# A four-layer graph network on one core: the tables that feed its list scheduler, and the order of its preparation, are replaced

## The reference

```python
deg_inv_sqrt = jnp.where(deg > 0, jax.lax.rsqrt(deg), 0.0)          # deg = adj.sum(axis=1)
x = _layernorm(x + norm_adj @ (x @ W0) + b0)                         # layer 0
o = softmax(mask(q @ k.T * scale)) @ v @ w_proj + b_proj             # layer 1: 8 heads, mask from adj
x = _layernorm(x + o + layernorm(o) * gamma + beta)
for _ in range(3):                                                   # layer 2: a gated unit, 3 steps
    z = sigmoid(av @ w3.T + h @ u3.T); r = sigmoid(av @ w4.T + h @ u3.T)   # av = [adj @ h, adj @ h]
    h = (1 - z) * h + z * tanh(av @ w5.T + (r * h) @ u5.T)
x = _layernorm(x + h)
x = _layernorm(x + softmax(q @ k.T / sqrt(32) + (1 - adj) * -1e9) @ v @ Wo + bo)   # layer 3
```

## Time and profile before

| what | value |
|---|---|
| median of 3 runs | 2582.63 us (2581.03 to 2584.98) |
| the profiled execution | 2584.22 us |
| its span in the trace | 2582.4 us, 1.8 us less than its own time |
| TensorE busy | 2531.3 us, 98% of the span |
| VectorE, ScalarE, GpSimd busy | 75%, 74%, 30% |
| mean granted TensorE clock | 0.997 |

### The profile page before, as it was taken

The page is one execution under the profiler, slowest core; times in us unless marked ns, Lnnn a source line. Parts: engine busy times, 40 slices in busy tenths (PEclk is TensorE's granted clock), DMA queues, the critical chain, the costliest instruction groups (busy, mean ns, idle before and its releaser), DMA issues.

```text
span 2582.4 us, 50299 instructions
## 1 busy us (share of the span) xinstructions
PE 2531.3 (98%) x17384; PEld 2052.0 (79%) x17384; DVE 1930.7 (75%) x5562; ACT 1913.1 (74%) x4322; POOL 775.7 (30%) x1086
## 2 busy tenths in 40 slices
PE   6999999999999999999999999999999999999997
PEld 5877787888878878788888888888788787787876
DVE  6867958769587785867868688695877858776776
ACT  3858848869597786968869597695977858684777
POOL 4323331323323222242323323233232322324221
PEclk9999999999999999999999999999999999999999
DMA  4212212122121222303122031221212223021122
GB/s 143 51 27 53 49 40 58 40 56 52 46 64 32 54 51 51 71 19 73 32 64 58 22 76 42 54 52 46 64 32 54 50 51 71 19 52 27 32 58 60
DMA packets 91083, 132.15 MB, mean 51 GB/s; under 512 B 15921, under 2 KB 40146, under 8 KB 90834
## 3 DMA queue, kind: packets, MB, share of 16 engines
q1 hardware_dynamic: 90834, 128.94, 21.0%
HBM read 19.83 MB, written 8.39 MB: 11 GB/s over the span
## 4 chain that ended last, share of the span: by engine, by line
PE 90%; DVE 5%; ACT 2%; issue 1%; POOL 1%; DMA 0%; SPq 0%; DVEq 0%; ACTq 0%; POOLq 0%
PE bank L1389 18%; PE bank L1390 17%; PE bank L1391 17%; PE bank L1446 16%; PE bank L1461 9%; PE bank L1438 8%; PE bank L1466 2%; PE bank L1499 1%; PE bank L1429 1%; ACT probs L940 1%; DVE probs L1179 1%; ACT res L977 1%; DVE PT L1190 0%; DVE vh L1245 0%; DVE gate L1156 0%
## 5 line engine op out<-in xcount | busy, mean ns | idle before, releaser
L940 ACT ACTIVATE probs<-probs,few 128x512 f32<-128x512 f32 x1024 | 731.4, 720 | 61.8 <-DVE few L1179 59.7
L1179 DVE CUSTOM_DVE_ANT_0 probs<-bank,mask 128x512 f32<-128x512 f32 x1024 | 668.5, 685 | 81.0 <-PE bank L1446 50.0
L1446 PE MATMUL bank<-ident,probs 128*128 128x128 f32 x4096 | 582.5, 273 | 7.4 <-ACT probs L940 5.3
L1446 PEld LDWEIGHTS bank<-ident,probs 128*128 128x128 f32 x4096 | 484.5, 141 | 84.1 <-issue 13.8
L1438 PE MATMUL bank<-stack 96*128 96x512 f32 x1024 | 419.8, 453 | 1.1 <-DMA stack<-qk 0.3
L949 ACT ACTIVATE PT<-bank 128x512 f32<-128x512 f32 x673 | 371.8, 596 | 37.1 <-PE bank L1446 31.6
L1190 DVE COPY PT<-bank 128x512 f32<-128x512 f32 x351 | 235.1, 682 | 49.4 <-PE bank L1466 30.5
L1389 PE MATMUL bank<-feat,W 128*128 128x512 f32 x640 | 259.1, 405 | 0.0
L846 POOL TENSOR_TENSOR feat<-o,feat 128x256 fp32r<-128x256 f32 x128 | 95.3, 744 | 527.6 <-ACT feat L962 526.3
L1390 PE MATMUL bank<-feat,W 128*128 128x512 f32 x640 | 253.3, 396 | 0.0
L1391 PE MATMUL bank<-feat,W 128*128 128x512 f32 x640 | 253.2, 396 | 0.0
(11 more groups left out here) (110 smaller groups left out, 5074.7 us busy)
## 6 DMA issues: line engine op xcount, KB each, us to landing
stack<-qk SPq DMA_DIRECT2D x768, 128.0 KB, 2.4
res<-in_x_dram SPq DMA_DIRECT2D x16, 512.0 KB, 3.8
out_dram<-res SPq DMA_DIRECT2D x16, 512.0 KB, 3.0
rows<-bo_sum SPq DMA_DIRECT2D x15, 128.0 KB, 2.9
rows<-in_L_gnn_bias_dram SPq DMA_DIRECT2D x14, 128.0 KB, 2.9
rows<-in_L_gnn_ln_beta_dram SPq DMA_DIRECT2D x14, 128.0 KB, 2.9
PT<-in_adj_dram SPq DMA_DIRECT2D x1, 1024.0 KB, 5.3
vh<-in_L_gnn_w_w_dram SPq DMA_DIRECT2D x2, 512.0 KB, 9.4
```

The lines of the kernel that those rows point to most:

```text
L940: k = act.activation(p, p, ACT.Exp, bias=least[:, t % P_RING:t % P_RING + 1], scale=-1.0, accum_out=sums[:, grp % 2, q * HG + h:q * HG + h ...
L1179: k = dve.tensor_tensor_reduce(out=probs[:, t % P_RING, :], in0=place("scores", t)[:, :], in1=mask[:, half * QT + q, :], scale=1.0, scalar ...
L1446: k = pe.transpose(place("transpose", t)[:, m * P:(m + 1) * P], probs[:, t % P_RING, m * P:(m + 1) * P], ident[:, :])
```

## The change

The numbers of the scheduler are replaced, and with them nearly every row of every engine's order moves. Beside that:

- `TO_PE`: TensorE sees what other engines produce 0.2 us later than others do, in the scheduler alone.
- `RANK` is another table, with kinds of its own for the first batches' pieces (`first ...`) and for each piece of preparation (`prep ...`).
- `mask3` is made on VectorE and the bias columns `cols` on GpSimd (each was on the other engine), and both masks come after batch 0 has been scaled.
- x of batch 2 is loaded with the first two. To free its place, the raw `u3` and `u5` lie in a part of `feat2` (`raw_us`); the first high half that overwrites it waits until they are turned.
- 17 transposes of the identity (`warm`), which no one reads, follow the row sums on TensorE.

```diff
+WARM = 17
-LATE = {"scores": 0.13, "stt": 0.11, "exp": 0.25, "transpose": 0.28, "pt": 0.25, "recip": 0.2, "rsum": 0.2, "values": 0.25,
+LATE = {"scores": 0.13, "stt": 0.11, "exp": 0.05, "transpose": 0.28, "pt": 0.13, "recip": 0.22, "rsum": 0.1, "values": 0.28,
+TO_PE = 0.2
-RAW_US = {"adj": (0.6, 4.6), "w0": (0.6, 2.5), "rows": (1.2, 2.0), "qkv1": (0.6, 3.5), "gru": (3.0, 5.0), "rest": (3.0, 5.0),
+RAW_US = {"adj": (0.6, 4.9), "w0": (0.6, 6.7), "rows": (1.2, 3.0), "qkv1": (0.6, 8.4), "gru": (4.0, 9.0), "rest": (4.0, 8.7),
...
-                ready = max([done[a] for a in piece.after], default=0.0)
+                late = TO_PE if piece.engines == ("PE",) else 0.0
+                ready = max([done[a] + (late if taken[a] != "PE" else 0.0) for a in piece.after], default=0.0)
                 if piece.opens:
-                    ready = max(ready, sorted(free)[len(piece.opens) - 1])
+                    ready = max(ready, sorted(free)[len(piece.opens) - 1] + late)
...
-    for name in ("adj", "x0", "w0", "x1", "qkv1", "rest", "gru", "small", "rows"):
+    for name in ("adj", "x0", "w0", "x1", "x2", "qkv1", "rest", "gru", "small", "rows"):
...
-    add("masks", "DVE", ("prep", "DVE", "mask1"), ("raw", "adj"))
-    add("masks_pool", "POOL", ("prep", "POOL", "mask3"), ("prep", "POOL", "pow"))
+    add("masks", "DVE", ("prep", "DVE", "mask1"), ("prep", "DVE", "dinv"), ("dve", "scale", 0, NT - 1))
+    add("masks", "DVE", ("prep", "DVE", "mask3"))
+
+    add("warm", "PE", ("prep", "PE", "warm"), ("prep", "DVE", "deg"), opens=[("warm", 0)], frees=[("warm", 0)])
...
-    add("biases", "DVE", ("prep", "DVE", "cols"), ("raw", "small"), ("raw", "rows"))
+    add("biases_pool", "POOL", ("prep", "POOL", "cols"), ("raw", "small"), ("raw", "rows"))
...
+                if name[:2] == ("ax", 2):
+
+                    wait_full(act, "turn", "u3")
+                    wait_full(act, "turn", "u5")
...
+                elif what == "warm":
+                    wait_free(pe, "warm", 0)
+                    pe.wait_ge(prep_pool.sem, prep_pool.at("ident"))
+                    pe.wait_ge(prep_dve.sem, prep_dve.at("some"))
+                    for i in range(WARM):
+                        k = pe.transpose(place("warm", 0)[:, 0:P], ident[:, :], ident[:, :])
+                    fill(k, "warm", 0)
```

More of the change, by code:

```diff
@@ new lines @@
+FIRST = ("scale", "ax", "w0", "n0", "rstd", "x1T", "q", "k", "v", "beta")
+def kind_of(key):
+    kind, what = key[:2]
+    if kind == "prep":
+        return f"prep {key[2]}"
+    if kind in ("pe", "act", "dve", "pool"):
+        b = key[2]
+        if what in FIRST and b < STREAMS and (what not in ("q", "k", "v") or key[3] == 1) and (
+                what != "rstd" or key[3] == "n0"):
+            return f"first {what} {b}" if what in ("scale", "ax", "w0") else f"first {what}"
+        return f"{kind} {what}"
+    if kind == "load" and what < STREAMS:
+        return "first load"
+    return f"values {key[2]}" if kind == "values" else kind
```

89 lines of the change are left out of this document (47 added, 42 removed), and 3 rows, old and new, of the table RANK.

## The result

The changed kernel takes 2589.73 us (median of 9 runs), the kernel before in the same comparison 2584.13 us (9 runs). The ratio is 1.0027, 95% interval 1.0018 to 1.0035: **slower by 0.27%**, where I had forecast 2575.5 us and given "slower" a chance of 0.11. The profiled execution has a span of 2587.9 us, 5.5 more than before. One of the nine runs took 3134 us at a mean granted clock of 0.751 and is left out of the ratio.

What follows compares the result with a forecast made beforehand. TensorE's order, idle time and half-clock work were taken to bound the kernel: 2582.4 - 8.3 + 3.3 - 0.5 - 1.5 = 2575.4 us of span, forecast as 2575.5 us. Range 2562 to 2585.

Steps and rivals of the forecast that it cites:

- slower: Rival, steady part: x3T waits as its chain gets 1.5 us longer, 12 batches lose 18: about 2593; chance 0.12.
- What bounds the kernel: Whole kernel: TensorE, busy 2531.3 of 2582.4 us; only its other 51 us and half-clock work can be won.
- that work was filler: Between batch 0's proj1 and x2T: TensorE work now done earlier had filled the norm chain; 6.0 us longer idle without it.
- a wait of over 5 us before batch 0's x2T: Sign expected in the profile after: TensorE waits that long ahead of these transposes.
- Start of ax: Opening: TensorE's first `ax` starts at 14.0 instead of 22.53, 8.5 us earlier.
- What is late next: Opening: weights wait for GpSimd's sums behind three scales from 23.2; w3 at 34.6, w5 at 39.2 us.
- Sum of the opening: Up to the first tile, at 65.0 with 12.1 us more work done: gain 8.3 us, bounds 11.2 or nothing.
- The middle of the opening: Batch 0's proj1 to x2T: 6.0 us more idle, 2.7 off for the norm; 3.3 us worse, bounds 0 and 6.
- Steady part: Repeating blocks: same TensorE work per batch, denser short blocks; 0.5 us better, bounds 6 either way.
- The end: Last block gets two more pieces of TensorE work, half of `proj3` moves later; 1.5 us better, bounds 0 and 3.
- It comes to nothing: Rival: scales cost near 6.22 us, or the chain to x2T is slow at half clock; say 2580; chance 0.26.
- two signs of being wrong: Bias row lands early in the opening, or a steady-part batch takes over 0.5 us longer.

Runs made afterwards that it cites:

- experiment 2: Kernel before with its own preparation, but the changed kernel's tables, ranks and later TensorE sight (`TO_PE`): 2593.0 us, ratio 1.0042.
- Experiment 1: Changed kernel plus one edge: q and k matmuls of layer 1 of batch 2 may not start before proj1 of batch 0: 2584.9 us, ratio 1.0009.
- Experiment 6: Changed kernel's preparation and opening ranks, with the kernel before's durations, delays and ranks for batch and tile work, `TO_PE` 0: 2581.9 us, ratio 0.9998.
- experiment 3: Changed kernel's preparation with the durations, delays and ranks of the kernel before: 2623.3 us, ratio 1.0161.
- experiment 7: Changed kernel with only TensorE's later sight (`TO_PE`) set from 0.2 to 0: 2639.0 us, ratio 1.0219.
- experiment 5: Kernel before plus one edge: proj1 of batch 0 waits for the last k matmul of layer 1 of batch 2: 2586.85 us, ratio 1.0016.

## Why the prediction was wrong

*What bounds the kernel* was right: TensorE's order and its idle time decide, and all differences lie there. The spent filler was named too, "that work was filler", and the sign to look for, "a wait of over 5 us before batch 0's x2T", is there with 5.42 us.

*Start of ax*: 14.0 forecast, 13.64 measured. *What is late next*: scales from 23.2 forecast, 23.6 measured; w3 at 34.6 against 32.94, w5 ready near 39.2 against sums that end by 36.7. I had added 2.9 us for shared time; the three scales took 7.95, 2.65 each instead of 2.40, so GpSimd lost 0.75 in all. VectorE lost more: its low halves of 0.67 took 2.40 and 2.27 beside the scales. The Trainium skill ("SBUF — State Buffer", section "SBUF: two separate sides") describes such a lock, held for a whole instruction; the trace agrees, with VectorE as the one that waits. *Sum of the opening*: 8.3 forecast, 11.2 measured, at the upper bound of 11.2. This step was mis-sized by 3 us in the safe direction, and only in part by the sums: `bv` stood ahead of w5 at half clock, so w5 was turned at 39.1 instead of 40.0. Batch 1's `w0` took 3.42 us instead of 5.1, since the granted clock was full again at 40.3, and u3 and u5 took 0.8 instead of 1.3. Of the 11.2 us 5.5 come with the new ranks and tables alone (experiment 2).

***The middle of the opening*, as I had priced it, held.** From `proj1` to `x2T` I took 3.3 us, with bounds of 0 and 6.0; the windows of block 1 give 2.0 (7.46 less 5.42). TensorE has 6.0 us less to do there, and the chain is 4.0 shorter, where I had taken 2.7 off for the norm. The wait of 5.42 looks like the whole answer, but before, the same stretch lost 5.4 us too, partly at half clock (granted clock 0.92).

**The first step that failed is one that is missing: between `x2T` of batch 0 and the steady part the sum has nothing.** There the changed kernel loses 5.4 us more in the rest of block 1, 5.0 in block 2 and 2.2 in block 3, 12.6 in all (blocks 0, 4 and 5 lose 1.6 less). "That work was filler" was carried only to the start of `x2T`. Behind it batch 0 goes on through further steps that wait for other engines (1.4 us for the low half at 137.6, 1.5 for the unit's state), TensorE is idle for 4.5 us instead of 1.6, and until 135.9 it works at the half clock that the wait had brought. Experiment 1 shows what the moved work is worth: with 6.8 us of it back, the stretch up to `x2T` loses 6.6 less and the rest of block 1 3.6 less, for 2.2 more ahead of `proj1` and 2.1 in block 0. Half clock is the smaller part: of the 15.8 us of block 1, 11.0 are idle and 4.8 slow work, against 4.6 and 3.1 in experiment 1, whose clock is full throughout that block; so it costs some 1.7.

Blocks 2 and 3 are another matter. Experiments 2 and 6 place their loss with the numbers of batch and tile work: 5.0 and 4.8 without the new preparation, 2.0 and 2.6 with it and the old numbers. Which of the ranks or delays does it I can't say: taken back in part, as in experiments 3 and 7, they give a worse order elsewhere. The rest of block 1 goes with something else: experiments 2 and 6, with the new and the old numbers of tile work, lose 9.1 and 8.6 us there, and experiment 3, without the new ranks of the opening, 2.2, as before.

*Steady part*: 0.5 better forecast, 1.0 worse measured over blocks 6 to 26, inside the bounds of 6. The short blocks of 45.07 us and the absent wait at x3T came as described, so the rival that ended slower did not cause the slowdown. *The end* is the second term that failed: 1.5 better forecast, 2.6 worse measured, outside the bounds of 0 and 3. I had counted the last block, which indeed lost 0.3 less (18.3 against 18.6); blocks 29 and 30 lost 2.3 and 3.7 us where they had lost 0.4 and 2.0. Experiment 6, with the old numbers, has 26.4 at the end: it too belongs to them. The sum as measured: -11.2 + 13.1 + 1.0 + 2.6 = 5.5, against -8.3 + 3.3 - 0.5 - 1.5 = -7.0.

The rival *slower* was the nearest in time, with 2593, and by luck: it put its loss at x3T in the steady part, where there is none. *It comes to nothing* had 2580, by too-dear scales or a slow chain; neither came. None of my cases let the opening gain and the blocks behind it lose more, and neither of my two signs of being wrong showed up.

## What to carry to other kernels

When an opening gets ahead by doing independent work early, look for the serial chain that this work used to cover, and follow it past the first stretch that you can price: here the stretch up to `x2T` lost 2.0 us more and the rest of the block 5.4. 6.8 us of moved matmuls were worth 8.1 us in that block, less the 2.1 that block 0 then lost, and one edge in the planner brought them back. Compare two orders by the loss of each stretch (length less work), not by length or by the steady part alone: here all but 1.0 of the 16.7 us given back lay outside it. A table and the ranks fitted with it belong together: setting back a single delay cost 49 us, and the old numbers on the new preparation ran 34 us above the changed kernel, so refit after every change of structure.

## What the runs showed of the hardware

I had not expected the clock to rise on transposes alone: in the changed kernel the 16 transposes of `adj` took 3.44 us (0.21 each) and the 17 that follow without a break 2.02 (0.12 each), so the clock had gone from 1.2 to 2.4 GHz before any other matmul had run. Without the 17, the last transpose of `adj` already came 0.12 behind the one before it; then, after 3.73 us of idleness, `ax` was back at half clock until 19.6. So the 17 did not raise the clock in the changed kernel but kept it up. The moment isn't fixed: in the kernel before, all 16 came 0.21 apart, and in experiment 5, with the same order, the last two 0.11. The Trainium skill ("TensorE: Matmul & The Clock Gate", Part 4) says that transposes don't raise the clock; for these fp32 transposes by matmul the trace shows otherwise. The earlier half-clock `ax` at 22.53 had a wait of 12.70 us before it and fits both.

A VectorE instruction of 0.67 us took 2.3 to 2.4 us beside a 2.65 us scaling on GpSimd, while the scaling itself lost only 0.25. It can go the other way: before, a scaling took 6.22 us beside VectorE.
